# A graph network on one core: dense blocks of 34 tiles from five regions of the edge list, in place of 24 tiles of one width

## The reference, cut to what matters

```
x: (12500, 128)   src, dst: 200000 edges, sorted by dst   edge_attr: (200000, 64)
dst = floor(12500 * u**2), u uniform: low nodes have most of the edges
h = relu(layernorm(x))
for layer in (1, 2):
    msg = concat([h[src], edge_attr]) @ W_msg.T
    agg = segment_sum(msg, dst, 12500)
    gi, gh = agg @ Wih.T + bih, h @ Whh.T + bhh
    r, z = sigmoid(i_r + h_r), sigmoid(i_z + h_z)
    n = tanh(i_n + r * h_n)
    h = (1 - z) * n + z * h
out = x + h
```

## Time and profile before

| | |
|---|---|
| median of three executions | 3468.92 us |
| profiled execution, its own time | 3465.33 us |
| its span | 3463.4 us |
| mean granted TensorE clock | 0.828 of full |
| PE busy | 2764.6 us, 80% |
| PEld busy | 2489.4 us, 72% |
| POOL busy | 2472.9 us, 71% |
| DVE busy | 1477.5 us, 43% |
| ACT busy | 1010.2 us, 29% |
| chain of waits, by engine | PE 37%, POOL 31%, issue 16%, DVE 5% |

### The profile page before, as it was taken

One profiled execution on the slowest core, in us unless ns is written; L12 is line 12 of the kernel. 1 busy time (PEld: TensorE's weight loads), 2 busy tenths in 40 slices (PEclk: granted clock), 3 DMA queues, 4 the chain that ended last, 5 costly groups with the idle time before them and its releaser, 6 DMA issues.

```text
span 3463.4 us, 74591 instructions
## 1 busy us (share of the span) xinstructions
PE 2764.6 (80%) x20436; PEld 2489.4 (72%) x20437; DVE 1477.5 (43%) x4429; ACT 1010.2 (29%) x2007; POOL 2472.9 (71%) x2544
## 2 busy tenths in 40 slices
PE   0788888988898998989867777778776878777886
PEld 0787877877887787778746767777776767766775
DVE  6543444444444444444423333333343444444443
ACT  5322222322233333332322122222222323233333
POOL 4677777777777777767527777777777777777772
PEclk9988888988988988988867677777787888888887
DMA  7333333333333333323233222222222222222221
GB/s 190 78 86 85 90 86 86 93 87 85 92 87 88 92 90 80 93 78 86 74 72 80 53 58 56 59 58 59 59 61 59 61 62 61 61 64 65 63 59 35
DMA packets 367262, 262.22 MB, mean 76 GB/s; under 512 B 239960, under 2 KB 325596, under 8 KB 366962
## 3 DMA queue, kind: packets, MB, share of 16 engines
q0 software_dynamic: 81376, 167.62, 17.8%
q1 hardware_dynamic: 264807, 70.52, 10.0%
q10 hardware_dynamic: 20779, 20.48, 2.0%
HBM read 239.14 MB, written 19.20 MB: 75 GB/s over the span
## 4 chain that ended last, share of the span: by engine, by line
PE 37%; POOL 31%; issue 16%; DVE 5%; ACT 3%; DMA 3%; DVEq 2%; ACTq 2%; POOLq 1%; SPq 0%
POOL rows L601 31%; PE ps_v L696 11%; PE ps_win L736 9%; PE ps_win L720 4%; PE ps_c L689 2%; PE ps_a L819 2%; PE ps_q L689 2%; DVEq L1093 1%; PE ps_c L823 1%; PE ps_c L821 1%; PE ps_b L824 1%; PE ps_d L826 1%; DMA rows<-h_table,idx 1%; ACT hr L1255 1%; PE ps_d L828 1%
## 5 line engine op out<-in xcount | busy, mean ns | idle before, releaser
L601 POOL DMA_INDIRECT rows<-h_table,idx x1252 | 1229.1, 982 | 481.9 <-issue 404.8
L601 POOL DMA_INDIRECT rows<-x_table,idx x1252 | 1219.0, 974 | 445.1 <-issue 433.9
L736 PE MATMUL ps_win<-onehot,rows 128*128 128x80 f32 x5008 | 801.8, 311 | 235.6 <-DMA rows<-x_table,idx 169.9
L736 PEld LDWEIGHTS ps_win<-onehot,rows 128*128 128x128 f32 x5008 | 716.8, 220 | 282.7 <-issue 169.2
L696 PE MATMUL ps_v<-hr,a_blk 125*120 125x128 f32 x5200 | 817.9, 330 | 0.0
L696 PEld LDWEIGHTS ps_v<-hr,a_blk 125*120 125x120 f32 x5200 | 796.8, 238 | 0.0
L1273 ACT COPY a_blk<-ps_q 125x390 f32<-125x390 f32 (+1 forms) x416 | 220.6, 530 | 1176.1 <-PE ps_q L689 1079.5
L1022 DVE SCALAR_TENSOR_TENSOR v_hot<-v_cur,lane 128x390 bf16<-128x390 f32 (+1 forms) x834 | 422.6, 544 | 0.0
L1101 DVE TENSOR_TENSOR aggT<-aggT,ps_win 128x80 f32 x626 | 143.8, 230 | 579.1 <-PE ps_win L736 520.8
L720 PE MATMUL ps_win<-onehot,attr 128*64 128x80 f32 x3128 | 317.7, 252 | 67.1 <-issue 44.0
L1036 DVE TENSOR_TENSOR onehot<-lane,rel 128x320 f32<-128x320 f32 x706 | 348.8, 494 | 24.2
(11 more groups left out here) (178 smaller groups left out, 1940.8 us busy)
## 6 DMA issues: line engine op xcount, KB each, us to landing
attr<-in_edge_attr_dram SPq DMA_DIRECT2D x390, 128.0 KB
rows<-h_table,idx POOLq DMA_INDIRECT x1252
rows<-x_table,idx POOLq DMA_INDIRECT x1252
dst_in<-in_dst_dram SPq DMA_DIRECT2D x702, 2.0 KB
idx<-in_src_dram SPq DMA_DIRECT2D x624, 2.0 KB
x_table<-out_sb ACTq DMA_DIRECT2D x50, 125.0 KB
attr<-in_x_dram ACTq DMA_DIRECT2D x50, 125.0 KB
out_dram<-out_sb ACTq DMA_DIRECT2D x50, 125.0 KB
```

What stands on the lines that cost most here:

```text
L601: nc.gpsimd.indirect_dma_start(out=rows[0:parts, s, j, :], out_offset=None, in_=table[:, :], in_offset=bass.IndirectOffsetOnAxis(ap=idx[0: ...
L736: mm = nc.tensor.matmul(ps_win[r % 2][:, 0:WIN], rows[0:parts, rr, j, :], onehot[0:parts, r % 2, j, :], start=(j == 0), stop=(j == TILES - 1))
```

## The change

A dense block takes 34 tiles from five regions of the dense part of the edge list. Region r has `n` tiles in each block, each with at most `w` targets, and `c` columns of the final window (`REGIONS`): 8 tiles of 2 targets, 7 of 3, 8 of 4, 7 of 5, 4 of 6, in all 128 columns for the counts and 128 for the window. There are 12 blocks, so 102 dense groups and 288 gathered ones with the rest; 12 x 4 steps in place of 52. The window's base is kept for each region, and `add_block` adds five pieces. The four packs of a slice hold regions (0, 1), (4), (2) and (3), with 15, 4, 8 and 7 tiles.

In layer 0 every fourth place of the order is an attribute-only group, 8 an iteration; the 6 that are left over (`HEAD`) are summed before the loop. Attributes and targets have a ring of 4 slots (`AR`) in place of 6; the ring of rows stays at 6. The rest's index load is issued without waiting for a slot. `ROT` is 4: the dense edges now reach node 849, so chunks 0 to 3 and 49 are the late ones. A chunk writes the new h to `z_sb`; PE turns it back behind the next chunk's message products; ACT copies h rows for the next chunk early. The tables at the start are made per region, with 4 blocks of 102 rows in place of 3 of 104. Of the diff, the overflow path, asserts, table layout and a part of the table arithmetic are cut.

```diff
-ITERS = 13
+ITERS = 12
...
-ROT = 2
-W = 5
-BT = RING * TILES
...
+ROT = 4
+AR = 4
+REGIONS = ((8, 2, 14), (7, 3, 20), (8, 4, 32), (7, 5, 36), (4, 6, 26))
+PACK_REGIONS = ((0, 1), (4,), (2,), (3,))
...
-    DENSE = ITERS * RING
+    DENSE = ITERS * BT // TILES
+    ATTR = SLOTS // (AR - 1)
+    HEAD = DENSE - ITERS * ATTR
     STEPS = ITERS * SUBS
...
-return [(q, None, q // 5) if q % 5 == 4 else (q, q - q // 5, None) for q in range(SLOTS + RING)]
+return [(q, None, q // AR) if q % AR == AR - 1 else (q, q - q // AR, None) for q in range(SLOTS + ATTR)]
...
-return it * len(order(layer)) + q
+return it * len(order(layer)) + q + (0 if layer else HEAD)
...
-return gi if layer else gi + gi // SUBS
+return gi if layer else gi + gi // (AR - 1)
...
+def slot(layer, q):
+return (q if layer else HEAD + q) % AR
+def attr_use(it, q):
+return it * ((SLOTS + ATTR) // AR) + (HEAD + q) // AR
...
-    sp.wait_ge(group_summed, p + (layer * ORDERED[0] - RING + 1 + AHEAD))
+    sp.wait_ge(group_summed, p + (layer * ORDERED[0] - AR + 1 + AHEAD))
...
-    for q, gi, ai in order(layer)[:RING]:
-        load_group(layer, 0, q, gi, ai)
     if layer == 0:
+        for p in range(AR):
+            load_edges(0, DENSE - HEAD + p, p)
...
+        for p in range(AR, HEAD):
+            slot_free(0, p)
+            load_edges(0, DENSE - HEAD + p, p % AR)
     else:
+        for q, gi, ai in order(layer)[:AR]:
+            load_group(layer, 0, q, gi, ai)
...
-    for r in range(2):
-        slot_free(layer, TAIL[layer] + r)
-        if r == 0:
...
-            sp.dma_start(idx[0:REST, 0, r, :], edges(src, FULL, REST)).then_inc(idx_loaded[0][r], 16)
+    sp.dma_start(idx[0:REST, 0, 0, :], edges(src, FULL, REST)).then_inc(idx_loaded[0][0], 16)
+    for k in range(2):
+        r = (TAIL[layer] + k) % AR
+        slot_free(layer, TAIL[layer] + k)
+        if k == 0 and layer == 0:
+            sp.dma_start(attr[0:REST, r, :, :].rearrange("p j d -> p (j d)"),
+                         edges(edge_attr, FULL, REST)).then_inc(attr_loaded[r], 16)
         sp.dma_start(dst_in[0:REST, r, :], edges(dst, FULL, REST)).then_inc(dst_loaded[r], 16)
...
-nc.gpsimd.iota(gidx[:, 0:DENSE], pattern=[[SUBS, ITERS], [0, RING]], base=SUBS, channel_multiplier=0, **small)
+nc.gpsimd.memset(gidx[:, 0:DENSE], float(STEPS))
...
-nc.gpsimd.iota(row_col[:, :], pattern=[[-W, BT]], base=0, channel_multiplier=1, **small)
+for r, (n, w, c) in enumerate(REGIONS):
+    nc.gpsimd.iota(row_col[:, tiles_of(r)], pattern=[[-w, n]], base=-ROW_AT[r], channel_multiplier=1, **small)
+    nc.gpsimd.memset(w_tile[:, tiles_of(r)], float(w))
+    nc.gpsimd.memset(per_w[:, r:r + 1], 1.0 / w)
+    nc.gpsimd.memset(less_w[:, r:r + 1], -(w - 1) / (2.0 * w))
+    nc.gpsimd.memset(reach[:, r:r + 1], c - w + 0.5)
+    nc.gpsimd.memset(col_at[:, r:r + 1], float(COL_AT[r]))
...
+for r, (n, w, c) in enumerate(REGIONS):
+    ins = nc.gpsimd.affine_select(out=row_of[:, tiles_of(r)], in_=row_of[:, tiles_of(r)], compare_op=ALU.is_ge, fill=0.0,
+                                  base=-ROW_AT[r], pattern=[[-w, n]], channel_multiplier=1)
+ins.then_inc(v_rows_made, 1)
...
-    wide = packed_cols(sl)
-    for j in range(PACK):
-        mm = nc.tensor.matmul((ps_q, ps_c)[k % 2][0:QUART, j * wide:(j + 1) * wide], lo_hot[:, k * PACK + j, :],
-                              v_hot[:, k % 2, j, 0:wide], start=True, stop=True)
+    for r, n, w, wide, at in pack_parts(sl, k):
+        for j in range(n):
+            own = slice(at.start + j * wide, at.start + (j + 1) * wide)
+            mm = nc.tensor.matmul((ps_q, ps_c)[k % 2][0:QUART, own], lo_hot[:, TILE_AT[r] + j, :],
+                                  v_hot[:, k % 2, own], start=True, stop=True)
     return mm
...
     def turn_back(cc):
-        pe.wait_ge(h_ready, cc)
+        pe.wait_ge(h_ready, cc + 1)
         pe.wait_ge(chunk_done, cc)
         for q in range(NQ):
-            tr = nc.tensor.transpose(ps_t[:, q * P:(q + 1) * P], halves(m_sb[:, :])[:, q, :], ident[:, :])
+            tr = nc.tensor.transpose(ps_t[:, q * P:(q + 1) * P], halves(z_sb[:, :])[:, q, :], ident[:, :])
         tr.then_inc(h_turned, 1)
...
         cc = layer * CHUNKS + i
         c = chunk_at(i)
-        with pe.If(i > 0):
-            turn_back(cc)
-        pe.wait_ge(h_rows_kept, cc + 1)
+        pe.wait_ge(t_ready, cc + 1)
+        pe.wait_ge(h_rows_kept, cc + (layer + 1))
         for q in range(NQ):
             tr = nc.tensor.transpose(halves(ps_h)[:, q, :], h_rows[:, q, :], ident[0:QUART, 0:QUART])
         tr.then_inc(hch_turned, 1)
         nc.tensor.matmul(ps_m, wT[:, layer, 0, :], cols(aggT, c), start=True, stop=False)
         nc.tensor.matmul(ps_m, wT[0:D, layer, 1, :], cols(edgeT[0:D, :], c),
                          start=False, stop=True).then_inc(msg_ready, 1)
+        with pe.If(i > 0):
+            turn_back(cc)
         pe.wait_ge(hch_kept, cc + 1)
         nc.tensor.matmul(ps_nh, wT[:, layer, 7, :], h_ch[:, :], start=True, stop=True)
...
+    if layer == 0:
+        for p in range(HEAD):
+            attr_group(p, p % AR, p // AR)
     with pe.Fori(0, ITERS) as it:
         blk = block_of(layer, it)
...
 dve.wait_ge(tiles_turned, 1)
-for to, ps in ((lo_t, ps_a), (hi_t, ps_b), (drel_t, ps_c)):
...
-nc.vector.tensor_reduce(v_max[:, :], tile_of, AX.X, ALU.max)
-chained(nc.vector.tensor_tensor(v_work, tile_of, row_col[:, :].unsqueeze(1).to_broadcast([VC, ITERS, BT]), ALU.add))
+for r, (n, w, c) in enumerate(REGIONS):
+    for to, ps in ((lo_t, ps_a), (drel_t, ps_c)):
+        nc.vector.tensor_copy(in_blocks(to[:, 0:NTILE])[:, :, tiles_of(r)], region_tiles(ps, r))
+    nc.vector.tensor_scalar(in_blocks(hi_t[:, 0:NTILE])[:, :, tiles_of(r)], region_tiles(ps_b, r), float(w), None, ALU.mult)
+    nc.vector.tensor_copy(in_blocks(tile_base)[:, :, tiles_of(r)], region_tiles(ps_d[0:1, :], r))
+    nc.vector.tensor_reduce(v_wide[:, :, r], region_tiles(ps_v[0:VC, :], r), AX.X, ALU.max)
+    nc.vector.tensor_reduce(v_min[:, :, r], region_tiles(ps_d[0:VC, :], r), AX.X, ALU.min)
+    nc.vector.tensor_reduce(v_max[:, :, r], region_tiles(ps_d[0:VC, :], r), AX.X, ALU.max)
+    nc.vector.tensor_reduce(region_of[:, r:r + 1], row_of[:, tiles_of(r)], AX.X, ALU.add)
...
+                                  row_col[:, tiles_of(r)].unsqueeze(1).to_broadcast([VC, ITERS, n]), ALU.add)
+chained(ins)
...
+nc.vector.tensor_tensor(v_max, v_max, v_min, ALU.subtract)
+nc.vector.tensor_tensor(v_from, v_min, each_block(col_at), ALU.subtract)
+nc.vector.tensor_tensor(v_wide, v_wide, each_block(per_w), ALU.mult)
...
-        lane[:, 0:QUART].unsqueeze(1).to_broadcast([P, PACK, QUART]),
-        block_cols(lo_t, it, k * PACK, PACK).unsqueeze(2).to_broadcast([P, PACK, QUART]), ALU.is_equal)
+    for r in PACK_REGIONS[k]:
+        n = REGIONS[r][0]
+        nc.vector.tensor_tensor(
+            lo_hot[:, tiles_of(r), :],
+            lane[:, 0:QUART].unsqueeze(1).to_broadcast([P, n, QUART]),
+            block_cols(lo_t, it, TILE_AT[r], n).unsqueeze(2).to_broadcast([P, n, QUART]), ALU.is_equal)
...
-        out=v_hot[:, k % 2, :, 0:wide],
-        in0=cur[:, k * PACK:(k + 1) * PACK].unsqueeze(2).to_broadcast([P, PACK, wide]),
-        scalar=float(slice_at[sl] * W),
-        in1=lane[:, 0:wide].unsqueeze(1).to_broadcast([P, PACK, wide]),
-        op0=ALU.subtract, op1=ALU.is_equal)
+    for r, n, w, wide, at in pack_parts(sl, k):
+        ins = nc.vector.scalar_tensor_tensor(
+            out=v_hot[:, k % 2, at].rearrange("p (t c) -> p t c", c=wide),
+            in0=cur[:, tiles_of(r)].unsqueeze(2).to_broadcast([P, n, wide]),
+            scalar=float(slice_at[sl] * w),
+            in1=lane[:, 0:wide].unsqueeze(1).to_broadcast([P, n, wide]),
+            op0=ALU.subtract, op1=ALU.is_equal)
+    return ins
...
     def add_block(it, blk):
...
-        a = aggT[:, bass.ds(at, XWIN)]
-        nc.vector.tensor_tensor(a, a, ps_v[:, 256:256 + XWIN], ALU.add).then_inc(acc_free, 1)
+        for r, (n, w, c) in enumerate(REGIONS):
+            a = aggT[:, bass.ds(starts[r], c)]
+            if r:
+                dve.drain()
+            ins = nc.vector.tensor_tensor(a, a, ps_v[:, 256 + COL_AT[r]:256 + COL_AT[r] + c], ALU.add)
+        ins.then_inc(acc_free, 1)
...
-        nc.vector.tensor_tensor(m_sb[:, :], m_sb[:, :], r_sb[:, :], ALU.add).then_inc(h_ready, 1)
-    for q in range(2):
-        onehot_of(q, gathered(0, q), q, dst_use(layer, 0, q))
+        nc.vector.tensor_tensor(z_sb[:, :], m_sb[:, :], r_sb[:, :], ALU.add).then_inc(h_ready, 1)
     if layer == 0:
+        for p in range(2):
+            onehot_of(p, DENSE - HEAD + p, p, 0)
+        for p in range(HEAD):
+            add_window(p, DENSE - HEAD + p, p % AR, P, False)
+            if p + 2 < HEAD:
+                onehot_of(p + 2, DENSE - HEAD + p + 2, (p + 2) % AR, (p + 2) // AR)
+            else:
+                q = p + 2 - HEAD
+                onehot_of(p + 2, gathered(0, q), slot(0, q), dst_use(0, 0, q))
         prepare(0)
         for k in range(2):
```

(32 more changed lines are left out.)

205 lines of the change are left out of this document (123 added, 82 removed).

## The result

The changed kernel takes **3339.0 us** (median of 4 runs, 3327.5 to 3340.0) against 3465.7 for the kernel before: ratio 0.963, interval [0.959, 0.967]. It is faster, as forecast, but 77 us short of the 3262 and outside the range of 3210 to 3325. The profiled execution spans 3337.5 us, 125.9 less than before (3463.4); the forecast's sum was 206.

The account below looks back on a forecast made before the run. POOL's gathers bound three quarters of layer 0 and all of layer 1, PE the last quarter of layer 0; -247 + 5 + 18 + 18 = -206 from 3465.3 gave 3259, 3262 us for the median, range 3210 to 3325.

Parts of the forecast that it names:

- The gathers that go: POOL, both layers: 96 fewer gathers in each save 124 and 123 us, -247 us, if PE lets POOL keep pace.
- What PE gets instead: PE in the blocks: added products mostly hidden in its waits, +20 us where PE-bound, chunks -14 us; sum +5 us.
- The first rival: Layer 0: PE takes over as the bound earlier than forecast; 3302 or 3387 us, chance 0.17.
- its mild form: Layer 0: half of its 1156 gathers run at PE's pace of 1.438 us, +40, so 3302 us.
- its full one: Layer 0: all gathers run at PE's pace of 1.438 us, +125, so 3387 us; chance 0.04 of the 0.17.
- DVE and the window's pieces: DVE in each block: more v_hot and lo_hot work and five window additions, taken as covered, 0 us.
- DVE slowing POOL: POOL's gathers: 7% more DVE work adds 0.002 us to each, +5 us at most, taken as 0.
- the prediction's rule against the change: Skill's rule that POOL contends with two-SBUF-input vector instructions, which v_hot and lo_hot are; sum 5 us worse by it.
- The start: Ahead of layer 0's loop: longer tables (+8) and six attribute sums (+10) lengthen POOL's wait, +18 us (12 to 34).
- Layer ends: Late chunks of both layers: five for three, periods of about 8 us for about 10, +18 us (+6 to +41).
- Rings of four, the index loads: Loads of attributes, targets and indices: they land in time, so no waits, 0 us.
- the second rival: PE's clock stays at 2.4 GHz, POOL's 39.0 us of waits go, late chunks take 6.5 us; 3206 us, chance 0.08.

Follow-up runs that it names:

- e15: Kernel of e11 with two of six slots gathering three tiles for four, PE's work kept: 3200.9 us, ratio 0.923.
- e13: Changed kernel with a block's window added in one piece, one value load and one DVE addition for five and five: 3306.6 us, ratio 0.954.
- e9: Changed kernel with lo_hot made once ahead of layer 0's loop and never again: 3298.4 us, ratio 0.953.
- the second profile: Changed kernel run again as it is, for a second profile and set of times: 3338.4 us, ratio 0.963.
- e16: Kernel before the change with one more two-input DVE comparison in every gathered group: 3559.0 us, ratio 1.026.
- e10: Changed kernel with one more one-input DVE operation of 32 x 320 elements in every gathered group: 3403.4 us, ratio 0.983.
- e8: Changed kernel with one more two-input DVE comparison of 32 x 320 elements in every gathered group: 3438.2 us, ratio 0.991.
- e1: Changed kernel with POOL filling slots 2 to 5 in layer 0's first iteration without waiting for row sums: 3325.3 us, ratio 0.958.
- e11: Kernel before the change with only the new chunk, turning back behind the next chunk's message products: 3400.4 us, ratio 0.981.
- e2: Changed kernel with the next iteration's six index loads spread over groups 18 to 23: 3331.8 us, ratio 0.960.
- e4: Changed kernel with two tiles of each region left out of the packs, 192 products a block for 272: 3370.1 us, ratio 0.970.
- e6: Kernel of e4 with 72 products a block added that nothing reads: 3347.5 us, ratio 0.964.
- e7: Changed kernel with 72 products a block added that nothing reads: 3357.6 us, ratio 0.968.

## Why the prediction was wrong

**The gathers that go.** 2 x 96 went and each layer was given its pace times 96, -124 and -123. In layer 1 this is nearly right: e15 measured 124 of 134 for its 105. In layer 0 it is the step that failed: "It counts in full if PE lets POOL keep its pace", and PE's 12% of idle time was taken for the room. Of PE's 182 us of idle time only the 60 of waits for rows were waits for POOL, 5 us a block where 10 were to be taken; of the 119 us forecast for this stretch (-124 + 5) 51 came. With its PE work kept and 105 gathers fewer, layer 0 gave 83 of 136 (e15), part of it through the clock. (The change differs from e15: with its thirteenth block go 100 products with hr and 24 groups' sums on PE.)

**What PE gets instead**: +5. "While POOL is the bound this lies in PE's waits." PE was without waits for rows from 500 us on, nine of twelve blocks, and POOL waited for it from 1000 us on, some five; the forecast had 3.2. Then POOL ran at 1.40 and 1.52 us a gather, slower than the 1.438 that the forecast knew. The first rival said that PE takes over earlier; its mild form gave 3302, its full one 3387, and the result lies between them. It deserved more than 0.17: the row for it, the waits of PE by who ended them, shows 60 us for rows and is not among the rows of the prediction.

**DVE and the window's pieces**: 0, "covered". This is the largest mis-sized term. PE's waits for DVE in the two lists go from 44 us to 97. Over the whole stretch they rose by 51. The pieces cost 32 us (e13), of which the forecast had priced 1.2 a block, and called them covered; it counted additions and not the loads of registers, for which the trace has no busy time, only "3.29 <-issue" at the first addition. lo_hot costs 41 us in all (e9), about half in each layer. How much of it is the ten tiles that were added wasn't measured; by tiles, ten of 34, it would be some 12, an estimate.

**DVE slowing POOL**: 0, at most 5. Measured 16 ns on each of 1156 gathers in layer 1 (13 in the second profile), 15 to 18 us, and 17 to 21 ns on each in layer 0, of which 7 to 11 us count before 1000 us. The gathers of 1900 to 2900 us, sorted by what DVE ran beside them, show where it comes from: with nothing beside, 275 of them take 0.946 us in the mean (0.944 before, 306 of them); beside v_hot alone 46 take 1.10, as before (51). The share of gathers with a DVE operation beside them is 64% for 61%. One of each kind:

```profile
1999.81 0.48 DVE L1112 SCALAR_TENSOR_TENSOR v_hot<-v_cur,lane 128x312 bf16<-128x312 f32 x1
1999.93 1.18 POOL L665 DMA_INDIRECT rows<-x_table,idx  x1 [0.31 <-issue]
...
2001.41 0.95 POOL L665 DMA_INDIRECT rows<-x_table,idx  x1 [0.30 <-issue]
```

The estimate took the lengthening as proportional to all of DVE's work, 0.002 us for 7% more; e9 shows 13 to 18 ns for lo_hot alone and e16 26 ns for 23% more DVE busy time, several times what the proportion gives. The Trainium skill (GPSIMD Engine Reference, section Specifications) has POOL contend with vector instructions of two SBUF inputs or in a mode that uses both ports. The trace agrees on the first in part: the prediction's rule against the change was real, and worth 15 to 18 us in layer 1 alone in place of the 5. In layer 1 up to 3250 us gathers beside v_hot or onehot alone take 1.13 and 1.12 us (18 and 21 of them), and those beside additions with one PSUM input 0.947 (23); but 11 beside `m_sb<-h_ch,r_sb`, with two SBUF inputs, take 0.947 too. The page's second case, a mode with both ports, can't be told from the runs: no run shows which mode an operation was in. The added operation with one input gave layer 1 the same mean as that with two (996 ns in e10, 997 in e8), but not gather by gather: over both layers, beside it alone 36 gathers take 0.97 us, 1.02 at most, and beside the two-input one 67 take 1.07, up to 1.25. What raised the mean of e10 as much isn't shown.

**The start**: +18, measured 28.9. The tables (+8.6) and the six sums (8) came as worked out. Missed was that `rows_free` counts HEAD's places, so POOL stands still with four slots empty: 13.7 us at the 25th gather (e1). It could be read from the code.

**Layer ends**: +18, measured +2.6. The period is 5.6 and 6.1 us, not 8: the forecast took the removed wait off (2.4) and kept the rest, but with the wait gone the granted clock among the late chunks is 0.98 for 0.66, and the products shrink with it (in e11, which has this edit alone, it is 0.89 from 1725 to 1745 us, with a period of 5.9). And the new chunk works inside layer 0, where it was given 14 us: 37 on the kernel before (e11). This part's surplus was luck for the forecast: without it the result would have been further off, near 3377, an estimate (23 us in layer 0 and 15 at the ends).

**Rings of four, the index loads**: 0. No wait on an attribute or target load appeared; the six index loads at once cost 7 us (e2).

**The range.** The lower ends of the terms (-15, +12 and +6 for +5, +18 and +18) add up to 38 us under the forecast, not 31. It changes nothing here: the miss is on the other side.

**The clock.** It is 0.85, 0.87 and 0.85 in layer 0, near the 0.87 and 0.86 of the earlier trace rows. Of the second rival the late chunks came true (5.6 us, it had 6.5); POOL's waits for PE didn't go. That added products are paid by the clock is true from e4 to e6 and not of e7. The Trainium skill (TensorE: Matmul & The Clock Gate, section What's actually happening) has the gate follow what PE did before; e4, where less work gave 0.78, agrees.

Open stays what the added packs cost. PE's pack products in layer 0 took 229 us before and 278 after by their rows, +49, against the forecast's 12 x 4.8 = 58; but e4 can't price what they cost the kernel, as the clock moved with them, and no other run leaves them out alone.

## What to carry to other kernels

An engine's idle time is room for another's speed-up only where the bound's data ends it: split it by releaser first. Here that was 60 us of 182. The clock can add to it (e15) or not (the change), which these rows didn't tell beforehand. Price register loads and drains beside the operations that they stand between, from the "issue" ahead of the first one. Where two engines are near the bound, a third one's work that stands ahead of either costs, busy share 45% or not; it can do so by lengthening the bound's own instructions (e16).

## What was not expected of the hardware

- Fewer matmuls made the kernel slower: 80 small products a block left out, clock 0.87 to 0.78, 31 us more; 72 idle ones put back, 0.86 and 23 us less.
- Five loads of a register on DVE take 3.29 us, more than the five additions that use them (1.5 us with their drains). One takes 0.45 us (e13).
- A gather is 0.94 to 0.95 us alone and up to 1.34 us beside one DVE operation, v_hot. Its mean over a layer goes from 974 to 1000 ns and from 982 to 1008 with one more comparison in each group (e16), and up to 1014 ns in layer 0 of e10.
